# Last graph-attention layer: one pass of 65-column products for source terms and residual, norm, values and ELU sum at other places

## The reference

```
Wh  = h @ W;  src = Wh @ a[:64];  dst = Wh @ a[64:]
e   = leaky_relu(src[:, None] + dst[None, :], 0.2), where adj > 0, else -9e15
z   = softmax(e, axis=-1) @ Wh + h @ W_res
z   = elu(z)
out = (z - mean(z)) * rsqrt(var(z) + 1e-5) * gamma + beta
```

## Time and profile before

| | |
|---|---|
| median of three runs | 3439.12 us |
| the profiled execution | 3440.61 us |
| its span, first to last instruction | 3438.8 us |
| TensorE, matmuls | 3028.6 us, 88% |
| VectorE | 3006.4 us, 87% |
| ScalarE | 2911.6 us, 85% |
| GpSimd | 994.5 us, 29% |
| mean granted TensorE clock | 0.97 of full |

### The profile page before, as it was taken

One profiled execution on the slowest core, in us unless ns is written; L12 is line 12 of the kernel. 1 busy time (PEld: TensorE's weight loads), 2 busy tenths in 40 slices (PEclk: granted clock), 3 DMA queues, 4 the chain that ended last, 5 costly groups with the idle time before them and its releaser, 6 DMA issues. The chain is left out here.

```text
span 3438.8 us, 78788 instructions
## 1 busy us (share of the span) xinstructions
PE 3028.6 (88%) x30972; PEld 1664.9 (48%) x30972; DVE 3006.4 (87%) x4666; ACT 2911.6 (85%) x3806; POOL 994.5 (29%) x869
## 2 busy tenths in 40 slices
PE   7997998999999979899898898998988989886875
PEld 5764666666666643333333333333333333335665
DVE  7886887887888889999999999999999999983666
ACT  4555887877878769999999999999999999994876
POOL 5433666666666620000000000000000000004786
PEclk9998999999999989999999999999999999996988
DMA  7640000000000000000000000000000000001221
GB/s 247 221 147 22 22 22 20 20 22 22 21 18 22 20 10 11 11 11 10 10 11 11 11 11 10 11 11 11 11 10 11 11 11 11 10 8 54 63 61 47
DMA packets 68412, 111.59 MB, mean 32 GB/s; under 512 B 26452, under 2 KB 26582, under 8 KB 68054
## 3 DMA queue, kind: packets, MB, share of 16 engines
q1 hardware_dynamic: 68054, 106.69, 10.1%
HBM read 86.61 MB, written 18.87 MB: 31 GB/s over the span
## 5 line engine op out<-in xcount | busy, mean ns | idle before, releaser
L1308 ACT ACTIVATE l_scalar_ring<-l_w,l_r 128x1024 f32<-128x1024 f32 x1568 | 1652.3, 1159 | 3.9 <-PEq L322 3.5
L1348 DVE TENSOR_SCALAR l_vector_ring<-l_w_code,l_r_code 128x2048 f32<-128x2048 f32 x1264 | 1602.6, 1340 | 3.1 <-PE scores L1240 0.6
L1230 PE MATMUL scores<-l_scalar_ring,l_signs 128*32 128x512 f32 x6272 | 750.6, 596 | 79.0 <-ACT l_scalar_ring L1308 78.5
L1240 PE MATMUL scores<-l_vector_ring,l_signs_code 128*32 128x512 f16 x10112 | 681.3, 392 | 105.1 <-DVE l_vector_ring L1348 103.2
L463 POOL TENSOR_TENSOR l_masked<-l_relu,mask 128x512 f32<-128x512 f32 x512 | 587.1, 1169 | 364.5 <-ACT l_relu L680 343.2
L172 POOL TENSOR_TENSOR stat<-stat,minus_half 128x8 f32<-128x8 f32 x32 | 70.5, 2203 | 1832.0 <-DVE stat L167 1831.9
L250 ACT COPY probs_t<-turned 128x512 f32<-128x512 f32 x448 | 256.1, 589 | 336.9 <-PE turned L209 336.9
L1240 PEld LDWEIGHTS scores<-l_vector_ring,l_signs_code 128*32 128x32 bf16 x10112 | 249.4, 95 | 566.4 <-DVE l_vector_ring L1348 232.5
L209 PE MATMUL turned<-ident,l_probs 128*128 128x128 f32 x3072 | 435.6, 287 | 35.6 <-ACT l_probs_t L1719 22.1
L277 ACT ACTIVATE l_probs<-l_logits,negmax 128x1024 f32<-128x1024 f32 x384 | 442.4, 1152 | 28.0 <-DVE negmax L268 28.0
L209 PEld LDWEIGHTS turned<-ident,l_probs 128*128 128x128 f32 x3072 | 344.6, 145 | 103.6 <-issue 90.4
(11 more groups left out here) (244 smaller groups left out, 2876.6 us busy)
## 6 DMA issues: line engine op xcount, KB each, us to landing
mask<-masks_kept SPq DMA_DIRECT2D x192, 256.0 KB, 2.6
l_adj<-adj SPq DMA_DIRECT2D x64, 512.0 KB, 5.9
masks_kept<-l_mask_ring SPq DMA_DIRECT2D x64, 256.0 KB, 5.0
x_res<-x SPq DMA_DIRECT2D x8, 256.0 KB, 4.8
out<-x_res SPq DMA_DIRECT2D x8, 256.0 KB, 2.6
l_h<-l_h SPq DMA_DIRECT2D x8, 128.0 KB, 2.8
l_kl<-l_dh SPq DMA_DIRECT2D x32, 2.0 KB, 1.7
l_kl<-l_dl SPq DMA_DIRECT2D x32, 2.0 KB, 1.9
```

The costliest lines, as they stand in the source:

```text
L1230: last = nc.tensor.matmul(s.scores[g * ROWS:(g + 1) * ROWS, buf, half, :], signs[:, window], scalar_ring[:, at % SCALAR_RING, g, halves[ha ...
L1240: last = nc.tensor.matmul(s.scores[g * ROWS:(g + 1) * ROWS, buf, half, :], signs_code[:, par, g % 2, window], parts(vector_ring[:, at % VE ...
L1308: last = nc.scalar.activation(scalar_ring[:, at % SCALAR_RING, g, :], w[:, par, :], ACT.Relu, bias=r[:, par, column:column + 1])
L1348: last = nc.vector.tensor_scalar(vector_ring[:, at % VECTOR_RING, g:g + 2, :], w_code[:, par, :, :], r_code[:, par, 0, column:column + 1], ...
```

## The change

- The input norm of graph b+2 goes one place sooner on each engine: centre at n = 2, square at n = 3, scale at n = 4, apply at n = 6. `out_centre` goes from n = 6 to n = 7.
- Fill 4 and the single-column source pass are replaced by one pass. `wres` gets a 65th column that holds the source weights, scaled by 0.8. `rest_of` multiplies four row blocks at a time by it, at n = 2 and at n = 3, just ahead of the unit's product, into columns 192 to 451 of the output bank. VectorE copies each half to `rest`, now 65 columns a block, right after it has the product (`take_rest`). The unit's output goes to columns 128 to 191. The relu's bias is column 64 of `rest`. ScalarE no longer takes a fill 4.
- `take_values` goes from n = 5 to n = 1, `elu_sum` and `out_mean` from n = 4 to n = 5, `out_seed` from n = 2 to n = 3.
- The waits follow: with K = 4 fills, masks and relus wait for fills 0 to 3, the relus of blocks 0 to 3 for the first half of `rest` and the others for the second; `finish` no longer waits for fill 4. At the layer's start the second half pass waits until the first is taken.

The diff, cut to its core:

```diff
-    K = 5
+    K = 4
+    HALF = NB // 2
...
-        rest = sb("rest", [P, 2, NB, D], F32)
+        rest = sb("rest", [P, 2, NB, D + 1], F32)
...
-        sources = s.outT[:, 3 * P:3 * P + NB]
-        unit_out = s.outT[:, P + D:P + 2 * D]
+        rest_bank = s.outT[:, P + D:P + D + HALF * (D + 1)].rearrange("p (a d) -> p a d", d=D + 1)
+        unit_out = s.outT[:, P:P + D]
...
 (gpsimd, mask)
-                g.wait_ge(sems["fill_copied"], fills_needed(b))
+                g.wait_ge(sems["fill_copied"], b * K + K)
 (gpsimd, graph)
-                    if n == 3 and norm:
+                    if n == 2 and norm:
                         layer_norm_centre(g, s, sems, next_norm(s, b), b + 2)
-                    if n == 4 and norm:
+                    if n == 3 and norm:
                         layer_norm_square(g, s, sems, b + 2)
                     if n == 5 and before > 1:
                         out_scale(b - 2)
-                    if n == 6 and before > 0:
-                        out_centre(b - 1)
-                    if n == 7 and norm:
+                    if n == 6 and norm:
                         g.wait_ge(sems["values_ready"], b + 1)
                         layer_norm_apply(g, s, sems, next_norm(s, b), par, b + 2, b * K + 2)
+                    if n == 7 and before > 0:
+                        out_centre(b - 1)
 (tensor)
-            def turn_sources(b, par):
+            def rest_of(b, par, half):
                 pe.wait_ge(sems["fill_copied"], b * K + 2)
-                for j in range(NB):
-                    last = nc.tensor.matmul(sources[:, j:j + 1], hT[0:D, par, j * P:(j + 1) * P], w_src[0:D, :], ...)
+                for j in range(HALF):
+                    block = half * HALF + j
+                    last = nc.tensor.matmul(rest_bank[:, j, :], hT[0:D, par, block * P:(block + 1) * P], wres[0:D, :], ...)
                 return last
...
-                    if n == 2 and project:
-                        turn_sources(b + 1, 1 - par)
+                    if n in (2, 3) and project:
+                        rest_of(b + 1, 1 - par, n - 2)
                     product(par, n, u)
...
-            turn_sources(0, 0).then_inc(sems["src_turned"], 1)
+            for half in range(2):
+                wait(pe, sems["src_ready"], half)
+                rest_of(0, 0, half).then_inc(sems["src_turned"], 1)
 (scalar)
-                    for k in takes_at(n, project, (0, 1, 4)):
+                    for k in takes_at(n, project, (0, 1)):
                         take_fill(b + 1, 1 - par, k)
 (vector)
+            def take_rest(par, half):
+                nc.vector.tensor_copy(rest[:, par, half * HALF:(half + 1) * HALF, :], rest_bank).then_inc(sems["src_ready"], 1)
...
                     v.wait_ge(sems["out_ready"], u + 1)
-                    if n == 2 and project:
-                        take_sources(1 - par)
+                    if n in (2, 3) and project:
+                        take_rest(1 - par, n - 2)
                     nc.vector.tensor_copy(turned_out[:], s.outT[:, 0:P]).then_inc(sems["out_copied"], 1)
                     for k in takes_at(n, project, (2, 3)):
                         take_fill(b + 1, 1 - par, k)
                     if n == 0 and norm:
                         layer_norm_mean(v, s, sems, next_norm(s, b), b + 2)
-                    if n == 2 and before > 1:
+                    if n == 1 and project:
+                        take_values(b + 1, 1 - par)
+                    if n == 3 and before > 1:
                         out_seed(b - 2)
-                    if n == 4 and before > 0:
+                    if n == 4 and norm:
+                        layer_norm_scale(v, s, sems, next_norm(s, b), b + 2)
+                    if n == 5 and before > 0:
                         elu_sum(b - 1, 1 - par)
                         out_mean(b - 1)
-                    if n == 5 and norm:
-                        layer_norm_scale(v, s, sems, next_norm(s, b), b + 2)
-                    if n == 5 and project:
-                        take_values(b + 1, 1 - par)
```

More of the change, by code:

```diff
@@ L1622, in fill @@
                     last = turn_y(pe, s, par, k, bank)
-                elif k < 4:
+                else:
                     last = nc.tensor.matmul(bank[:], w_dst[0:D, :], hT[0:D, par, cols], start=True, stop=True)
-                else:
-                    for j in range(NB):
-                        last = nc.tensor.matmul(bank[:, j * D:(j + 1) * D], hT[0:D, par, j * P:(j + 1) * P], wres[0:D, :],
-                                                start=True, stop=True, skip_group_check=True)
                 last.then_inc(sems["fill_ready"], 1)
-            def turn_sources(b, par):
+            def rest_of(b, par, half):
                 pe.wait_ge(sems["fill_copied"], b * K + 2)
-                for j in range(NB):
-                    last = nc.tensor.matmul(sources[:, j:j + 1], hT[0:D, par, j * P:(j + 1) * P], w_src[0:D, :], start=True, stop=True,
-                                            skip_group_check=True)
+                for j in range(HALF):
+                    block = half * HALF + j
+                    last = nc.tensor.matmul(rest_bank[:, j, :], hT[0:D, par, block * P:(block + 1) * P], wres[0:D, :], start=True,
+                                            stop=True, skip_group_check=True)
                 return last
@@ L1700, in take_fill @@
                 a.wait_ge(sems["fill_ready"], b * K + k + 1)
[L1701 to L1704, removed]
+                last = nc.scalar.activation(hT[0:D, par, cols], bank[0:D, :], ACT.Relu)
                 last.then_inc(sems["fill_copied"], 1)
             def take_relu(b, par, n):
-                a.wait_ge(sems["fill_copied"], fills_needed(b))
-                a.wait_ge(sems["src_ready"], b + 1)
+                a.wait_ge(sems["fill_copied"], b * K + K)
+                a.wait_ge(sems["src_ready"], 2 * b + 1 + n // HALF)
                 wait(a, sems["logits_ready"], STARTS + b * NB + n - 1)
-                nc.scalar.activation(relu[n % 2], dst_slope[:, par, :], ACT.Relu, bias=src[:, par, n:n + 1],
+                nc.scalar.activation(relu[n % 2], dst_slope[:, par, :], ACT.Relu, bias=rest[:, par, n, D:D + 1],
                                      scale=1.0 / SLOPE - 1.0).then_inc(sems["relu_ready"], 1)
@@ L1747, in graph @@
                         elu_power(b - 1)
-            for k in (0, 1, 4):
+            for k in (0, 1):
                 take_fill(0, 0, k)
@@ L1880, in _ @@
             nc.vector.tensor_copy(w_dst[0:D, :], s.outT[0:D, 0:P])
-            nc.vector.tensor_copy(w_src[0:D, :], s.outT[0:D, P:P + 1]).then_inc(sems["weights_ready"], 1)
+            nc.vector.tensor_scalar(wres[0:D, D:D + 1], s.outT[0:D, P:P + 1], 1.0 - SLOPE, None, ALU.mult).then_inc(sems["weights_ready"], 1)
             for k in (2, 3):
                 take_fill(0, 0, k)
-            v.wait_ge(sems["src_turned"], 1)
-            take_sources(0)
+            for half in range(2):
+                v.wait_ge(sems["src_turned"], half + 1)
+                take_rest(0, half)
             take_values(0, 0)
```

18 lines of the change are left out of this document (5 added, 13 removed).

## The result

The changed kernel took 3408.49 us (median of 4 runs, 3407.82 to 3412.32) against 3437.96 us of the kernel before beside it (3436.32 to 3444.52): a ratio of 0.9913 with a 95% interval of 0.9896 to 0.993, 29.5 us less where 23.3 were forecast. Between the profiled executions the spans differ by 32.2 us.

The account below looks back on a forecast made before the run. No engine is full; each graph of the last layer is a chain that changes hands between engines. Terms -1.9 - 5.3 - 7.5 - 8 - 2.6 + 2 = -23.3 took 3439.1 to 3416 us, range 3404 to 3429.

Parts of the forecast that it names:

- Norm, -7.5: GpSimd's chain from dst_slope to y shortens to 13.2 us; the first fill's four waits for y go: -7.5 us.
- Start, -2.6: At the layer's start two half passes replace residual and source passes in series: -2.6 us.
- Passes, -1.9: Units 1 to 4: source and residual passes out, two half passes in; -0.27 us a graph, 7 graphs: -1.9 us.
- p(3) to p(4): From the start of unit 3's product to unit 4's: set by VectorE, 3.7 us instead of 4.14, -0.44.
- Values, -5.3: take_values leaves unit 5 for unit 1, hidden behind VectorE's wait for TensorE: 0.76 us in 7 graphs, -5.3 us.
- crowding, +2: Denser GpSimd work meets VectorE's two-operand SBUF operations more often: from 0 to +5 us, taken as +2.
- Clock, -8: Falls of TensorE's clock right behind the single-column source pass go: zero to 10.8 us, three quarters taken, -8.
- Rivals 1 and 5: 1: clock keeps falling at dense units, 3424 us, chance 0.20; 5: it falls in units 4 to 7, 3460, 0.05.
- Rival 2: GpSimd, nearly gapless beside VectorE, lengthens four VectorE operations in 6 graphs: +10 us, 3426 us, chance 0.13.
- Rival 3: ScalarE's relu of the next graph's first unit waits for dst_slope, 1.3 us later: +9 us, 3425 us, chance 0.10.
- the second: Sign of being wrong: TensorE's wait for VectorE's finish (L1800) grows beyond 28.5 us.
- the third: Sign of being wrong: ScalarE's wait for dst_slope grows by a microsecond per graph.

Follow-up runs that it names:

- e8: The changed kernel with out_seed moved from unit 3 to unit 1, behind the values: 3404.28 us, ratio 0.9906.
- e9: The changed kernel with take_values back in unit 5, behind the ELU sum: 3415.89 us, ratio 0.9932.
- e1: The kernel before with each of the eight source products 32 equal columns wide instead of one: 3435.53 us, ratio 0.9987.
- e6: The changed kernel with an extra pass of eight 60-column products in unit 2, ahead of the half pass, results unused: 3436.97 us, ratio 0.9993.
- e11: The kernel before with its single-column source pass cut into four products in unit 2 and four in unit 3: 3435.07 us, ratio 0.9991.
- e4: The kernel before with the passes alone changed: two 65-column half passes in units 2 and 3, no fill 4, seed in unit 3: 3433.7 us, ratio 0.9987.
- e12: The changed kernel with values and seed in unit 0 and the norm's mean in unit 1: 3421.9 us, ratio 0.9948.
- e2: The kernel before with the norm one place sooner, the scale in unit 4 and the ELU sum in unit 5: 3429.68 us, ratio 0.9974.
- e3: The kernel before with take_values in unit 1 instead of 5, nothing else: 3442.38 us, ratio 1.001.
- e10: The kernel before with norm, ELU sum and values moved, but old source pass, fill 4 and seed in unit 2: 3423.19 us, ratio 0.9949.
- e5: The changed kernel with an extra pass of eight one-column products in unit 2, ahead of the half pass, results unused: 3437.68 us, ratio 0.9997.
- e7: The changed kernel with the norm back at its old places and the ELU sum back in unit 4: 3423.19 us, ratio 0.996.

## Why the prediction was right, and where not

The direction, the range (3404 to 3429) and the terms for norm and start held; the forecast was 7.5 us too high. That it was no further off is in part luck: the clock gave some 11 us more than forecast, the values 2 less, and the passes' term is right in its sum alone. Step by step:

- **Norm, -7.5:** -7.75, of which some 0.9 was clock. The four waits are gone, and GpSimd's chain has the length worked out (13.1 for 13.2). Its idle time was sized wrongly (4.5 us, not 3), without effect.
- **Start, -2.6:** -2.45.
- **Passes, -1.9:** -1.8, but from other places. In graphs 0 and 1, where nothing is seeded, p(1) to p(4) fell from 13.2 to 12.1; in the other five it rose from 13.35 to 13.45. The step that failed is p(3) to p(4), priced at 3.7 us in all seven graphs. It is 2.79 in the two without a seed and 4.15 in the five with one. The seed's price came from a series of unit 2 (2.09 us), in which the small operation behind the reduction stands with 0.17 us and GpSimd idle; moved beside a mask it takes 0.68. That is the missing half microsecond, and e8 confirms it from the other side.
- **Values, -5.3, with crowding, +2:** some -1.4 for -3.3. In graph 1 the move gives 0.9 us, in graph 3 0.02, and in graph 6 it costs some 0.7. e9 suggests that its larger part is indirect: with the values in unit 5, behind the ELU sum, there are falls from between p(6) and p(7) on that the change doesn't have.
- **Clock, -8:** some -19 by the estimate above, of which -10.7 at the place forecast (the bound was 10.8). This is the term that was mis-sized: three quarters of one set of falls was taken, and the falls of units 4 to 7, which stood in the range's lower end with 5 us, gave some 8 (why they went is shown by no run). And its cause was wrong: the prediction named single columns, and e1, e6 and e11 take that away. What these runs show to matter is whether the thin pass stands in one piece.
- **The rivals.** Rivals 1 and 5 are refuted: no fall behind a half pass, and two short ones in units 4 to 5. Rival 2 is right in its mechanism (values 1303 ns) and wrong in its price, for the longer values lie in VectorE's idle time. What the prediction held against it, a mean of 0.76 us beside masks, showed only that VectorE had started first. The traces agree with the rule of the port pair in the Trainium skill (page "SBUF — State Buffer", section "SBUF: two separate sides"), that whichever engine starts first holds the pair for its whole instruction: 0.68 against 1.48 us for the values. Rival 3 happened (up to 1.5 us in each graph), and its price is shown by no run: e8 has the same wait in total, 10.4 us, in graphs of 30.8 us, so it isn't what held the changed kernel's graphs at 31.9.
- **The Trainium skill's rule of short idle gaps** (page "TensorE: Matmul & The Clock Gate", section "A second HAM failure mode: psum-queue depth-cycling") would have made the term 0; it was not: TensorE's waits for VectorE grew from 28.5 to 37.1 us while its time at the lower clock fell from 44.4 to 6.8. The falls in e4 and e12 do come with waits of TensorE, of 3.8 and 3.0 us. Those of the earlier trace rows and of e1 come after 3.8 to 5.1 us without a gap, and the gap ahead of that, 0.85 us in unit 1, stands in e11 too, which doesn't fall there.
- **My own signs.** Of the three that were to prove me wrong, the second came true (the wait for VectorE's finish, 37.1 us for 28.5), and the third came near (the wait for dst_slope grew by 0.7 us a graph, not 1), while the time fell by more than forecast. The second contradicted my own sum: 3.7 us from p(3) to p(4) with the residual pass out of 4.14 leaves TensorE 1.5 us of waiting in every graph.

Open: with the pass in one piece (the kernel before, e1, e2, e3, e10) 19 of 35 graphs fall behind it, with 16 extra records ahead of the half pass (e5 and e6) 5 of 14, and with the pass split (the changed kernel, e4, e7, e8, e9, e11, e12) none of 49, one of which (graph 3 of e12) was at the lower clock already. Why only about half of the unsplit ones fall isn't shown. Nor is the split of -9.2 more than an estimate from a few graphs.

## What to carry to other kernels

Parts of a change that lie on one loop aren't added up: what the others give is seen only after the binding wait (here y) is gone, and alone each may look worthless (3442, 3434) that is worth 7 to 15 us in company. Find the binding loop first, and test parts by leaving one out of the whole rather than by adding one to the kernel before. When a step is moved, price every instruction of it by the slack of its new unit, and look at what the other engine holds there: against the best version, the seed in unit 3 cost 4 us, and values and seed in unit 0 cost 17.6.

## What was not expected of the hardware

- A pass of 16 records in a row, 64x1 or 64x32 each, was followed by a fall of TensorE's clock from 2.4 to 1.2 GHz in about half of the graphs, and one of 24 with 64x1 or 64x60 in a third (5 of 14), with TensorE busy without a gap; eight at a time were never followed by one (48 graphs).
- With each wait of TensorE of 3.0 to 3.9 us behind the layer's start a fall came, inside the wait or within 1.2 us of its end (11 waits for y in the kernel before, e1, e3, e4, e7 and e11, and three for VectorE in e12); with the waits for y of 0.8 to 1.3 us none did. A fall lasted 3.4 or 6.8 us, and once 20.5, with TensorE busy 20.6 of 21 us (e12): a late operand was paid several times over.
- VectorE's operation on 128x8 took 0.68 us when a mask addition of GpSimd had begun 0.5 us before it, and 0.17 us with GpSimd idle: it ended with the addition. A row of 512 took 0.68 us when it started first and 1.48 when it started 0.2 us into the addition.
